# Chosen experts addressed by registers, and the closing work of a mixture-of-experts block in fused VectorE operations

## What is computed

```python
def _L1_ffn_ref(x, Wr, br, W1, b1, W2, b2, gamma, beta):      # x is _ln_t(t)
    logits = jnp.mean(x, axis=1) @ Wr + br                    # one row for each image
    routing_weights = jax.nn.softmax(logits, axis=-1)
    expected_loads = routing_weights.sum(axis=0) * (N / B)
    scale = jnp.where(expected_loads > capacity, capacity / expected_loads, 1.0)
    routing_weights = jax.nn.softmax(routing_weights * scale, axis=-1)
    rw_tok = jnp.broadcast_to(routing_weights[:, None, :], (B, S, E)).reshape(N, E)
    top_w, top_i = jax.lax.top_k(rw_tok, K)                   # K = 2 of E = 8
    top_w = jax.nn.softmax(top_w, axis=-1)
    h = jax.nn.gelu(jnp.einsum('nd,edf->enf', xf, W1) + b1[:, None, :], approximate=False)
    y = jnp.einsum('enf,efd->end', h, W2) + b2[:, None, :]    # 128 -> 256 -> 128
    ...
    out = jnp.einsum('ne,end->nd', w_dense, y).reshape(B, S, D)
    return _layer_norm(out + x, gamma, beta)
t = t + _L1_ffn_ref(_ln_t(t), ...)
```

## Time and profile before

| what | us |
|---|---|
| median of three runs (3835.17 to 3839.79) | 3836.81 |
| the profiled execution | 3838.61 |
| its span, first to last instruction | 3836.5 |
| last block, 3598.1 to the end | 238.4 |
| normalise and transpose, 3603.2 to 3626.3 | 23.1 |
| route, 3626.3 to 3651.2 | 24.9 |
| select for image 0, 3651.2 to 3670.3 | 19.1 |
| experts, 3670.3 to 3817.9 | 147.6 |
| after the last product, 3817.9 to the end | 18.6 |

### The profile page before, as it was taken

The page is one execution under the profiler, slowest core; times in us unless marked ns, Lnnn a source line. Parts: engine busy times, 40 slices in busy tenths (PEclk is TensorE's granted clock), DMA queues, the critical chain, the costliest instruction groups (busy, mean ns, idle before and its releaser), DMA issues. The chain is left out here.

```text
span 3836.5 us, 97899 instructions
## 1 busy us (share of the span) xinstructions
PE 3551.4 (93%) x30782; PEld 2678.6 (70%) x30782; DVE 2785.7 (73%) x6801; ACT 2080.6 (54%) x3661; POOL 1448.0 (38%) x671
## 2 busy tenths in 40 slices
PE   7759999999999999999999999999399999999776
PEld 4437777777777777777777777777277777778555
DVE  6858777777777777877777777778465555644598
ACT  3336666666666666666666666666145454545433
POOL 2335555555555555555555555555100000000223
PEclk8879999999999999999999999999699999999788
DMA  5444224223224223322422422221520111000001
GB/s 168 140 116 105 80 90 123 89 84 106 88 87 126 88 67 101 110 86 95 110 74 95 118 89 88 70 87 60 158 79 14 40 54 40 1 1 0 28 13 38
DMA packets 122409, 307.36 MB, mean 80 GB/s; under 512 B 15609, under 2 KB 85292, under 8 KB 101548
## 3 DMA queue, kind: packets, MB, share of 16 engines
q1 hardware_dynamic: 122284, 305.78, 25.8%
...
## 5 line engine op out<-in xcount | busy, mean ns | idle before, releaser
L729 DVE CUSTOM_DVE_ANT_0 c_S<-c_Sps,mask_tiles 128x768 f32<-128x768 f32 x1728 | 1607.5, 955 | 531.8 <-PE c_Sps L781 521.1
L670 ACT ACTIVATE c_PT<-c_Tps 128x512 f32<-128x512 f32 x2592 | 1457.6, 602 | 927.4 <-PE c_Tps L792 861.4
L642 POOL TENSOR_SCALAR c_S<-c_S,c_row_max 128x2304 f32<-128x2304 f32 x576 | 1264.4, 2195 | 1195.6 <-DVE c_row_max L740 1195.6
L792 PE MATMUL c_Tps<-ident,c_S 128*128 128x128 f32 x10368 | 1457.8, 274 | 4.1 <-ACT c_PT L670 4.1
L792 PEld LDWEIGHTS c_Tps<-ident,c_S 128*128 128x128 f32 x10368 | 1219.7, 140 | 261.1 <-issue 119.1
L781 PE MATMUL c_Sps<-c_K,c_Q 96*128 (+1 forms) x3456 | 853.6, 328 | 59.2 <-DMA c_Q<-q_parts 40.9
L805 PE MATMUL c_Ops<-c_PT,c_V 128*32 128x256 f32 x10368 | 648.8, 383 | 0.8 <-ACT c_PT L670 0.8
L781 PEld LDWEIGHTS c_Sps<-c_K,c_Q 96*128 96x128 bf16 x3456 | 325.5, 98 | 209.5 <-issue 136.0
L805 PEld LDWEIGHTS c_Ops<-c_PT,c_V 128*32 128x32 f32 x10368 | 304.6, 109 | 222.4 <-ACT c_PT L670 46.4
L1242 DVE TENSOR_SCALAR_CACHE_REDUCE l_S<-l_Sps 128x384 f32<-128x384 f32 x432 | 240.5, 558 | 270.7 <-PE l_Sps L1089 242.7
L1019 ACT ACTIVATE l_PT<-l_Tps 128x384 f32<-128x384 f32 x432 | 196.5, 491 | 395.2 <-PE l_Tps L1110 395.2
...
## 6 DMA issues: line engine op xcount, KB each, us to landing
...
```

The source lines that it names most:

```text
L642: pool.tensor_scalar(S[:, slot, :], S[:, slot, :], -1.0, row_max[:, slot:slot + 1], ALU.mult, ALU.add).then_inc(shifted, 1)
L670: act.activation(dst, src, ACT.Exp, scale=-1.0).then_inc(exp_done, 1)
L729: dve.tensor_tensor_reduce(out=S[:, r % ROW_SLOTS, cols(CH, c)].rearrange("p (k n) -> p k n", k=2), in0=Sps[:, n % S_SLOTS, :, 0:GW], in1= ...
L792: last = pe.transpose(Tps[:, g % T_SLOTS, cols(P, k)], S[:, (2 * b + t) % ROW_SLOTS, cols(P, kt)], ident[:, :])
```

## The change

Only `layer1_ffn` is touched.

- The routing now gives each image's two expert numbers and two weights (`routed`, four numbers in place of 40). They are spread over the partitions as `sel`, and cast to integers as `experts`. DVE and ACT each read the two numbers of an image into registers (`value_load`).
- `select(b)` copies the two chosen blocks of `W1`, scales the two chosen of `W2`, and forms `b2s` from two rows. GELU's bias is read from `b1` at the register's place.
- `base` and `residual` (adding `beta` to `x1`) are on DVE, one operation for each image. Closing goes by groups: `close`, `statistics`, `aggregate`, then `centre` ((y - mean) * gamma in one operation for each tile) and `finish` (times the reciprocal deviation, plus the residual).
- GpSimd raises variance + 1e-5 to the power -0.5, once for all 72 tiles at the start of the block and once for each group of three. The square roots on ACT and the reciprocals on DVE are gone. GpSimd also builds `pick` and `index` at the start.
- DVE takes a third of the transposes (groups 4 and 5 of each image); they have four slots. `1/N` is multiplied into `Wr`.
- The loops are unrolled, and SP stores each group (24 stores of 192 KB in place of 8 of 576 KB).

```diff
+            for b in range(B):
+                for g in range(NG):
+                    sp.wait_ge(out_ready, NG * b + g + 1)
+                    sp.dma_start(out[b][:, cols(GB, g), :], ln[:, cols(GB, NG * b + g), :]).then_inc(out_stored, 16)
+            sp.wait_ge(out_stored, 16 * GROUPS)
...
+            pool.memset(power[:, :], -0.5).then_inc(rstd_step, 1)
+            pool.tensor_scalar(rstd[:, :], moments[:, :, 1:2].rearrange("p t a -> p (t a)"), 1e-5, None, ALU.add).then_inc(rstd_step, 1)
+            pool.wait_ge(rstd_step, 2)
+            pool.tensor_tensor(rstd[:, :], rstd[:, :], power[:, :], ALU.pow).then_inc(rstd_ready, 1)
             pool.memset(ones[:, :], 1.0).then_inc(constants, 1)
...
             pool.memset(greater[:, :, :], 0.0).then_inc(constants, 1)
...
-            pool.wait_ge(ln_ready, NG * B)
-            with pool.Fori(0, B) as b:
-                for half in range(2):
-                    last = pool.tensor_tensor(tokens(x1, b, half), tokens(x1, b, half), everywhere(beta[:, :, :]), ALU.add)
-                last.then_inc(res_ready, 1)
...
-                for half in range(halves):
-                    pool.wait_ge(y_normed, 2 * b + half + 1)
-                    alone(pool)
-                    pool.tensor_tensor(tokens(ln, b, half), tokens(ln, b, half), everywhere(gamma[:, :, :]), ALU.mult).then_inc(scaled, 1)
-                    pool.wait_ge(res_ready, B)
-                    pool.wait_ge(scaled, 2 * b + half + 1)
-                    alone(pool)
-                    pool.tensor_tensor(tokens(ln, b, half), tokens(ln, b, half), tokens(x1, b, half), ALU.add).then_inc(out_ready, 1)
...
+            for e in range(E):
+                last = pool.memset(index[:, :, e:e + 1], float(e))
+            last.then_inc(constants, 1)
+            pool.wait_ge(constants, 3)
+            for b in range(B):
+                last = pool.tensor_scalar(pick[:, b, :], ones[0:B, :], ident[0:B, b:b + 1], None, ALU.mult)
+            last.then_inc(constants, 1)
+            for n in range(GROUPS):
+                pool.wait_ge(y_moments, n + 1)
+                pool.tensor_scalar(yrstd[:, n % 2, :], ymv[:, n % 2, :, 1:2].rearrange("p t a -> p (t a)"), 1e-5, None, ALU.add).then_inc(rstd_step, 1)
+                pool.wait_ge(rstd_step, n + 3)
+                pool.tensor_tensor(yrstd[:, n % 2, :], yrstd[:, n % 2, :], power[:, 0:GB], ALU.pow).then_inc(yrstd_ready, 1)
...
-            act.wait_ge(constants, 3)
-            act.activation(sd[:, :], moments[:, :, 1:2].rearrange("p t a -> p (t a)"), ACT.Sqrt, bias=eps[:, :]).then_inc(sd_ready, 1)
...
+                    act.wait_ge(t_ready, n + 1)
+                    act.activation(lnT[:, b, cols(GW, g)], Yps[:, n % T_SLOTS, 0:GW], ACT.Copy,
+                                   accum_out=sums[:, b, g:g + 1]).then_inc(t_taken_act, 1)
...
+            act.wait_ge(experts_ready, 1)
+            act.wait_ge(small_taken, 3)
+            for n in range(GROUPS):
+                b, g = divmod(n, NG)
+                if g == 0:
+                    expert = [act.value_load(experts[0:1, b, k:k + 1], min_val=0, max_val=E - 1) for k in range(TOPK)]
...
                     act.wait_ge(y_ready, n - 1)
                 for i in range(HK):
                     act.wait_ge(h_ready, HK * n + i + 1)
-                    act.activation(hid[:, g % 2, i, :], Hps[:, i, 0:GW], ACT.Gelu,
-                                   bias=b1s[:, b % 2, i // FH, i % FH:i % FH + 1]).then_inc(h_taken, 1)
...
-                act.wait_ge(yvar_ready, b + 1)
-                act.activation(ysd[:, :], ymv[:, :, 1:2].rearrange("p t a -> p (t a)"), ACT.Sqrt, bias=eps[:, :]).then_inc(ysd_ready, 1)
+                    act.activation(hid[:, n % 2, i, :], Hps[:, i, 0:GW], ACT.Gelu,
+                                   bias=b1[:, bass.ds(expert[i // FH], 1), i % FH:i % FH + 1].rearrange("p e n -> p (e n)")).then_inc(h_taken, 1)
...
-            pe.wait_ge(constants, 3)
+            pe.wait_ge(constants, 4)
...
+                pe.wait_ge(ln_ready, n + 1)
+                slot_free(pe, n)
+                for k in range(GB):
+                    last = pe.transpose(Yps[:, n % T_SLOTS, cols(P, k)], ln[:, n * GB + k, :], ident[:, :])
...
+                    dve.wait_ge(t_ready, n + 1)
+                    dve.tensor_scalar(lnT[:, b, cols(GW, g)], Yps[:, n % T_SLOTS, 0:GW], 1.0, None, ALU.mult, ALU.add,
+                                      accum_out=sums[:, b, g:g + 1]).then_inc(t_taken_dve, 1)
+
+            LAG = 2
+            for n in range(GROUPS + LAG):
+                if n < GROUPS:
+                    for t in tiles_of(n):
+                        last = dve.tensor_scalar(ln[:, t, :], x1[:, t, :], moments[:, t, 0:1], rstd[:, t:t + 1],
+                                                 ALU.subtract, ALU.mult)
+                    last.then_inc(ln_ready, 1)
+                if n >= LAG:
+                    take_transposes(n - LAG)
...
-            for b in range(B):
-                dve.tensor_scalar(pick[:, b, :], ones[0:B, :], ident[0:B, b:b + 1], None, ALU.mult)
-            step(dve.tensor_scalar(means[:, :], means[:, :], 1.0 / N, None, ALU.mult))
+            dve.tensor_scalar(Wr[:, :], Wr[:, :], 1.0 / N, None, ALU.mult)
+            dve.wait_ge(t_taken_act, by_act(GROUPS))
+            dve.wait_ge(t_taken_dve, GROUPS - by_act(GROUPS))
+            step(dve.tensor_reduce(means[:, :], sums[:, :, :], AX.X, ALU.add))
...
+            dve.tensor_tensor(r[:, 11:11 + TOPK, :], choice[:, :, :], index[:, :, :], ALU.mult)
...
+            step(dve.tensor_reduce(rc[:, 11:13], r[:, 11:11 + TOPK, :], AX.X, ALU.add))
+            step(dve.tensor_scalar(routed[:, 0:TOPK], rc[:, 11:13], float(E - 1), None, ALU.min))
...
-            step(dve.tensor_tensor(choice[:, 2 * TOPK, :], choice[:, TOPK, :], choice[:, TOPK + 1, :], ALU.add))
+            step(dve.reciprocal(routed[:, TOPK:TOPK + 1], rc[:, 10:11]))
+            step(dve.tensor_tensor(routed[:, TOPK + 1:TOPK + 2], routed[:, TOPK:TOPK + 1], rc[:, 9:10], ALU.mult))
...
+            dve.tensor_copy(sel[:, :, :].rearrange("p b s -> p (b s)"), Yps[:, 2, 0:B * ROUTED])
+            dve.tensor_copy(experts[:, :, :].rearrange("p b s -> p (b s)"), Yps[:, 2, 0:B * ROUTED]).then_inc(experts_ready, 1)
+            dve.wait_ge(experts_ready, 1)
...
-                if layer == 0:
-                    jobs = [(w1s[:, t, k, :], W1[:, e, :], of(k)) for k in range(TOPK)]
-                    jobs += [(b1s[:, t, k, :], b1[:, e, :], of(k)) for k in range(TOPK)]
-                else:
-                    jobs = [(w2s[:, t, k, :], W2[:, e, :], of(TOPK + k)) for k in range(TOPK)]
-                    jobs.append((b2s[:, t, :], b2[:, e, :], of(2 * TOPK)))
...
-                        last = dve.tensor_scalar(dst, src, factor, None, ALU.mult)
-                    else:
-                        last = dve.scalar_tensor_tensor(out=dst, in0=src, scalar=factor, in1=dst, op0=ALU.mult, op1=ALU.add)
-                last.then_inc(select_step if e < E - 1 else (selected_1, selected_2)[layer], 1)
...
+                expert = [dve.value_load(experts[0:1, b, k:k + 1], min_val=0, max_val=E - 1) for k in range(TOPK)]
+                for k in range(TOPK):
+                    last = dve.tensor_copy(w1s[:, b % 2, k, :], W1[:, bass.ds(expert[k], 1), :].rearrange("p e n -> p (e n)"))
+                last.then_inc(w1_taken, 1)
+                for k in range(TOPK):
+                    last = dve.tensor_scalar(w2s[:, b % 2, k, :], W2[:, bass.ds(expert[k], 1), :].rearrange("p e n -> p (e n)"),
+                                             sel[:, b, TOPK + k:TOPK + k + 1], None, ALU.mult)
+                last.then_inc(w2_scaled, 1)
+                dve.tensor_scalar(b2s[:, b % 2, 0, :], b2[:, bass.ds(expert[0], 1), :].rearrange("p e n -> p (e n)"),
+                                  sel[:, b, TOPK:TOPK + 1], None, ALU.mult).then_inc(half_bias, 1)
+                dve.wait_ge(half_bias, 2 * b + 1)
+                dve.scalar_tensor_tensor(out=b2s[:, b % 2, 0, :], in0=b2[:, bass.ds(expert[1], 1), :].rearrange("p e n -> p (e n)"),
+                                         scalar=sel[:, b, TOPK + 1:TOPK + 2], in1=b2s[:, b % 2, 0, :],
+                                         op0=ALU.mult, op1=ALU.add).then_inc(half_bias, 1)
...
+            def base(b):
+                dve.wait_ge(half_bias, 2 * (b + 1))
+                image = ln[:, cols(TILES, b), :]
+                dve.tensor_tensor(image, image, b2s[:, b % 2, :, :].to_broadcast([P, TILES, C]), ALU.add).then_inc(base_ready, 1)
+
+            def residual(b):
+                image = x1[:, cols(TILES, b), :]
+                dve.tensor_tensor(image, image, beta[:, :, :].to_broadcast([P, TILES, C]), ALU.add).then_inc(res_ready, 1)
...
-            def finish(b):
-                variances(b, NG - 1).then_inc(yvar_ready, 1)
-                dve.wait_ge(ysd_ready, b + 1)
-                dve.reciprocal(yrstd[:, :], ysd[:, :]).then_inc(y_step, 1)
```

(45 more changed lines are left out.)

275 lines of the change are left out of this document (87 added, 188 removed).

## The result

The changed kernel takes 3792.6 us (median of 4 runs, 3790.4 to 3793.7), the kernel before, beside it on the same chip, 3838.3 us (median of 4, 3835.2 to 3842.6). The ratio is 0.988, 95% interval 0.986 to 0.989: 45.7 us faster. The forecast was 3781.3 us in a range of 3774 to 3803; the time lies in the range, 11.3 us above the forecast. The profiled execution has a span of 3791.0 us against 3836.5 before.

What follows compares the result with a forecast made beforehand. The block was read as bound in turn by DVE's chain, DVE's selection, PE, DVE at each border, and the closing work. Terms +1.9 + 1.1 - 14.4 - 35.6 - 8.5 = -55.5 us gave 3781.3 us, range 3774 to 3803.

Steps and rivals of the forecast that it cites:

- large term: End of routing to last product: 166.7 us falls to 131.1, -35.6 us, only if DVE keeps up.
- routing: Chain of small steps: `pick`, the scaling and GpSimd's hold-up leave it, -14.4 us, 10.5 us left.
- power at the head: Block's start: GpSimd's power over 72 columns, ahead of PE's first product, put at 2.5 us, at most 10.
- start: Head of the block: DVE's reciprocal goes, -0.6, and PE waits for GpSimd's power, +2.5; +1.9 us.
- transposes: Normalise and transpose stage: DVE becomes late with eight groups from PSUM, 24.2 us, +1.1 us.
- closing: After the last product: closing by groups takes 10.1 us in place of 18.6, -8.5 us.
- Rival 1: Experts: GpSimd's power over three columns delays `centre`, so DVE becomes the bound; 3802 us, chance 0.15.
- Rival 2: Selection: register loads take 4 us each, delaying the first product and DVE's images; 3796 us, chance 0.09.
- third rival: Head of the block: the 72-column power is so slow that the kernel loses; 3851 us, chance 0.06.
- rule against the change: `centre` and `finish`: DVE operations with two SBUF inputs wait out GpSimd's; 3.16 us seen in place of 0.88.
- DVE's share: Experts: DVE's rounds of 3.2 us, wide operations and selection fill 28.6 of an image's 31.6 us.
- borders: Between images: PE stands still, 10.05 us at the first, behind DVE's 11.65 us of `finish` and selection operations.

Runs made afterwards that it cites:

- e5: Changed kernel with the old amount of selection work put back on DVE (other seven experts added with factor zero); 3839.7 us.
- e4: Kernel before with seven eighths of the selection left out, closing work still on DVE and GpSimd; 3818.5 us.
- e1: Changed kernel with the power over 72 columns replaced by a square root on ACT and a reciprocal on DVE; 3779.0 us.
- e2: Changed kernel with the 72-column power moved behind the constants and cut into four parts, one for each image; 3779.4 us.
- e3: Changed kernel with `residual` back on GpSimd, as eight additions behind the normalising; 3805.6 us.
- e6: Changed kernel with `centre` and `finish` of six groups held back to the image's end, still on DVE; 3795.7 us.

## Why the prediction was right, and where it failed

**The large term held.** From the end of the routing to the last product I had put 131.1 us, 2.6 to the first product and 128.5 for the experts, and the trace has 2.3 and 128.9. Its condition was that DVE keeps up. Run e5 shows that it is one: with DVE busy for 39.5 us an image, more than the 31.6 that PE needs, the gain is gone.

**The two parts of the change need each other.** The stage from the end of the routing to the last product shows it without the head and the routing, which e5 shares with the changed kernel. It takes 166.7 us before and 131.2 after. Without most of the selection's work but with the old closing work it takes 146.0 (e4). With the new closing work but the old selection's amount it takes 178.7 (e5), 12 us more than before. So in this stage the closing work on DVE is a loss with the old selection, and pays only with the short one. I had added the terms up without saying so; the text had the pieces, the row of 3.16 us among them, but not that either part alone leaves PE waiting.

**The step that failed is the power at the head.** I had put 2.5 us for 72 columns and 10 as the upper bound, on the ground that the addition of the same shape is cheap. It took 11.91 us, beyond my bound, and 29 times the addition of the same 72 columns just ahead of it (0.41). That is 9.4 of the 10.0 us missing from the sum. The rest of the start is 1.2 us more than I had put, mostly the four `pick` rows, at 0.59 each, which I had counted with the fills. The block's first instruction came 1.3 us later, in blocks that the change doesn't touch, and the transposes and the closing gave 2.1 back. The last 1.3 us of the 11.3 lie between the span and the median: I had put the median 0.3 us above the span, and it is 1.6 above. Runs e1 and e2 settle the cause: two different ways of getting the power out of the chain give 3779.0 and 3779.4.

**That the time lies in the range is luck.** The power at my bound of 10 us gave 3789, and the measured 3792.6 lies beyond it. The range went on to 3803 only for the sake of rivals 1 and 2, neither of which came.

The mistake in method: a row of another operation on the same engine bounded nothing, and the operation could have been moved off the chain whatever it cost. The third rival, a power so slow that the kernel loses, named the right place; it decides at 0.8 us a column, and the power takes 0.165 (11.91 / 72).

**The transposes** were bound by DVE, as I said, 22.64 of 23.1 us, and took 23.1 in place of 24.2. I had put 0.65 us for each of the eight groups that DVE takes from PSUM; in the chain they stand with 0.47 to 0.57, and DVE's work is 22.64 us in place of 23.8. PE's clock was granted at 0.50 before and at 0.72 on average now. DVE is busy for nearly the whole stage, so this changed nothing.

**The routing** came to 10.6 us against 10.5, but the number is right by a wrong split. I had counted 8.58 us of `pick` and 2.52 of the scaling as work that leaves the chain, and only 2.55 as the effect of `residual` leaving GpSimd, on two operations of 1.15 and 1.81 us. These now stand in the chain with 0.23 and 0.17:

```profile
3641.68 0.23 DVE e_r L1585
...
3642.67 0.17 DVE e_r L1590
```

Run e3, which puts `residual` back, has 1.05 and 1.79 there again. But it also makes the way from the sum over the tokens to the spread numbers 23.9 us, where the kernel before had 24.9 and the changed one 10.6, though `pick` and the scaling are out of its chain. The additions then catch other operations in their place. This row of the kernel before says why:

```profile
3622.19 20.59 POOL L1450 TENSOR_TENSOR x<-x,e_beta 128x1152 f32 x8 [23.66 <-DVE e_ln L1596]
```

Each of the eight additions takes 2.57 us on average. Taken as equally long, the second to the fifth of them end at 3627.3, 3629.9, 3632.5 and 3635.1, and `pick`'s four operations last from 3626.57 to 3635.15; the scaling and the two operations of 1.15 and 1.81 us end at 3637.7, 3640.3 and 3642.8, each with the next addition. So nearly all of the routing's gain is due to GpSimd's additions being gone. My rule against the change named only operations with two inputs in SBUF; `pick`, the scaling and seven of the eight caught in e3 have one tensor as input.

**DVE's share was overestimated.** I had 28.6 us of DVE's work in an image of 31.6; the stretch inside the images has DVE busy for 23.70 of 31.5. A round takes 2.9 us in place of 3.2, from `close` at 3700.31 to the end of `centre` at 3703.21, and the selection with its two loads 2.1 us (3703.21 to 3705.28) where I gave it 4. It did no harm, but it made rival 1 look nearer than it was.

**Rival 1** had the power hold up `centre`, deciding from 1.15 us. The two small operations together last 1.19 us (from 3701.96 to 3703.15), so by its own numbers it stood at its threshold. It did not come, for another reason: the power does not hold up `centre`. The timeline has the power over three columns and `centre` at the same time:

```profile
3702.28 0.87 POOL L1457 TENSOR_TENSOR e_yrstd<-e_yrstd,e_power 128x3 f32<-128x3 f32 x1
3702.35 0.86 DVE L1676 SCALAR_TENSOR_TENSOR e_ln<-e_ln,e_ymv,e_gamma 128x128 f32<-128x128 f32 x3
```

`centre` runs at its full pace. **Rival 2**, register loads of 4 us, is out: two loads with all their work are 1.5 us, where I had chosen 2.0.

**The borders.** I had read the stand-still as DVE's row of `finish` and the selection behind it. Run e6 sets the row apart: 9.4 us of closing work in a row don't stop PE. The row stretched by GpSimd, with no selection behind it, costs PE 1.28 us at the third border before and nothing in e4. With seven small operations behind it, which wait for GpSimd, PE stops for 5.91 us, and with the old selection for 10.05 and 9.65. GpSimd's additions are not the only way to such a stop: in e5 there are no such additions, and the amount of DVE's work alone stops PE for 9.7 us. No run takes the additions away and leaves the rest of the kernel before as it was, so what they cost by themselves in the 10.05 us isn't shown.

A stop of PE costs more than its length. After the stops of 10.05 and 9.65 us the next row of `outputs` takes 4.89 and 5.34 us in place of 2.68, at granted clocks of 0.58 and 0.52. From the first `hidden` to the last product the kernel before takes 156.9 us and the changed one 128.9. Of these 28.0 us, 22.8 are PE's waits (10.05, 9.65, 1.28 and 1.77 ahead of the first `outputs`), and nearly all the rest is such slow rows behind them.
